# Cross attention with image tokens on one core: the transposes of x placed between the scores and the output projection, and copied out in the same step

## What is computed

```python
q = heads(x @ W_q);  k_t, v_t = heads(text @ W_k), heads(text @ W_v)
probs_t = softmax(q @ k_t.T * scale)                    # 73 text tokens
text_out = probs_t @ v_t
k_ip, v_ip = heads(ip @ W_k_ip), heads(ip @ W_v_ip)     # 4 image tokens
sem = l2norm(probs_t @ text) @ l2norm(ip).T
probs_ip = softmax(q @ k_ip.T * scale + 0.5 * sem) * spatial_mask
out = (text_out + probs_ip @ v_ip) @ W_out + b_out + x
```

## Time and profile before

| | |
|---|---|
| median of 3 runs | 1068.55 us (1067.39 to 1069.84) |
| the profiled execution, its own time | 1065.76 us |
| its span in the profile | 1063.6 us |
| mean granted clock of TensorE | 0.984 of full speed |
| busy: PE, DVE, ACT, POOL | 93%, 77%, 64%, 56% |

### The profile page before, as it was taken

The page is one execution under the profiler, slowest core; times in us unless marked ns, Lnnn a source line. Parts: engine busy times, 40 slices in busy tenths (PEclk is TensorE's granted clock), DMA queues, the critical chain, the costliest instruction groups (busy, mean ns, idle before and its releaser), DMA issues.

```text
span 1063.6 us, 23677 instructions
## 1 busy us (share of the span) xinstructions
PE 988.4 (93%) x7637; PEld 800.9 (75%) x7637; DVE 816.2 (77%) x2397; ACT 677.0 (64%) x1995; POOL 590.6 (56%) x1570
## 2 busy tenths in 40 slices
PE   5996587899998999999998999999999999999967
PEld 4872466688887888888877888888877888888745
DVE  3246378988888888888887888888888888888762
ACT  1124368776776776767766676777766777776630
POOL 0000347766666666756665666666655666666650
PEclk9899799999999999999999999999999999999999
DMA  9598558988889888879798988878898988787852
GB/s 281 167 184 207 124 119 172 156 173 174 168 177 183 172 189 170 184 156 189 156 174 170 185 182 172 174 169 168 167 189 174 188 171 184 142 162 142 156 127 93
DMA packets 484393, 180.56 MB, mean 170 GB/s; under 512 B 451228, under 2 KB 462334, under 8 KB 484271
## 3 DMA queue, kind: packets, MB, share of 16 engines
q1 hardware_dynamic: 484271, 179.07, 81.9%
HBM read 42.74 MB, written 27.22 MB: 66 GB/s over the span
## 4 chain that ended last, share of the span: by engine, by line
PE 73%; DMA 7%; DVE 3%; issue 2%; POOL 2%; ACT 2%; SPq 1%; POOLq 0%; DVEq 0%; ACTq 0%
PE ps_Q L1095 24%; PE ps_O L1061 24%; PE ps_S L1034 11%; PE ps_U L1081 11%; DMA pts<-ph 6%; PE ps_M L1109 3%; ACT pr L818 1%; POOL ph L902 1%; SPq L706 1%; DVE bias L939 1%; ACT ph L830 0%; DMA x_in<-in_x_dram 0%; DMA ipT<-ip 0%; DVE smax L932 0%; DVE pr L972 0%
## 5 line engine op out<-in xcount | busy, mean ns | idle before, releaser
L818 ACT ACTIVATE pr<-ps_S,bias 128x73 f32<-128x73 f32 x1280 | 288.7, 337 | 141.2 <-DVE bias L939 141.2
L902 POOL TENSOR_TENSOR ph<-pr,ph 128x440 f16<-128x440 f32 x320 | 227.8, 733 | 209.2 <-ACT ph L830 209.0
L1061 PE MATMUL ps_O<-wo_hi,aT 128*128 128x320 f16 x1280 | 293.2, 300 | 6.1 <-DVE x_in L924 4.1
L1095 PE MATMUL ps_Q<-xT,wq_hi 128*128 128x512 f32 x800 | 279.8, 415 | 7.0 <-DVE qT L909 6.1
L830 ACT ACTIVATE ph<-pr 128x584 f16<-128x584 f32 x320 | 204.2, 688 | 5.6 <-DMA pts<-ph 0.6
L1061 PE MATMUL ps_O<-wo_lo,aT 128*128 128x320 f16 x640 | 191.3, 299 | 0.0
L1081 PE MATMUL ps_U<-xm,pts 128*128 128x110 f16 (+1 forms) x2560 | 156.6, 213 | 26.4 <-DMA pts<-ph 24.8
L1081 PEld LDWEIGHTS ps_U<-xm,pts 128*128 128x128 f16 (+1 forms) x2560 | 143.4, 98 | 44.4 <-DMA pts<-ph 25.2
L1034 PE MATMUL ps_S<-kbd,qT 128*128 128x308 f32 x960 | 169.7, 312 | 2.8 <-ACT pr L818 2.7
L1095 PEld LDWEIGHTS ps_Q<-xT,wq_hi 128*128 128x128 f32 x800 | 146.0, 190 | 34.9 <-DVE qT L909 7.9
L1061 PEld LDWEIGHTS ps_O<-wo_hi,aT 128*128 128x128 f16 x1280 | 124.8, 98 | 62.9 <-DVE x_in L924 4.8
(11 more groups left out here) (175 smaller groups left out, 1307.0 us busy)
## 6 DMA issues: line engine op xcount, KB each, us to landing
out_dram<-x_in SPq DMA_DIRECT2D x64, 320.0 KB, 3.1
x_in<-in_x_dram SPq DMA_DIRECT2D x60, 320.0 KB, 3.5
w_k<-in_L_xattn_W_k_dram SPq DMA_DIRECT2D x5, 512.0 KB, 9.4
w_ip<-in_L_xattn_W_k_ip_dram SPq DMA_DIRECT2D x1, 2560.0 KB, 12.0
w_v<-in_L_xattn_W_v_dram SPq DMA_DIRECT2D x1, 2560.0 KB, 20.2
w_ip<-in_L_xattn_W_v_ip_dram SPq DMA_DIRECT2D x1, 2560.0 KB, 10.6
pts<-ph SPq DMA_TRANSPOSE x160, 4.4
xm<-x_d SPq DMA_DIRECT2D x20, 110.0 KB
```

What stands on the lines that cost most here:

```text
L818: last = nc.scalar.activation(pr[p % P_RING][:, j, h, :], sc[:, j, h, 0:T], ACT.Exp, bias=bias[p % 2][:, j, h:h + 1], scale=SCALE)
L902: nc.gpsimd.tensor_tensor(lo, full[:, :, t0:t1], one[:, :, 0, t0:t1], ALU.subtract).then_inc(pl_ready, 1)
L1061: last = nc.tensor.matmul(o_bank[half % 2][:, 0:HALF], stationary, moving, start=(k, a, b_) == O_MMS[0], stop=(k, a, b_) == O_MMS[-1])
L1095: last = nc.tensor.matmul(ps_Q[:], wq[a][:, c, k * P:(k + 1) * P], xT[(CC * i + c) % XT_RING][b_][:], start=(c, a, b_) == Q_MMS[0], stop=( ...
```

## The change

On PE the transposes of x are placed behind the scores and ahead of the output projection. ACT and DVE copy them out in the same step, at the same place in their order. The last two chunks of a tile are transposed one step later (places 7 and 8 instead of 6 and 7), so they are copied out in the same steps as before. The first three are transposed in the same steps as before and copied out one step earlier.

```diff
-    XT_AT = {-10: 0, -9: 1, -8: 2, -4: 3, -3: 4}
+    XT_AT = {-10: 0, -9: 1, -8: 2, -3: 3, -2: 4}
...
@@ scalar @@
-                for j, c in x_at(p - 1):
+                for j, c in x_at(p):
                     act.wait_ge(xT_ready, CC * j + c + 1)
...
@@ tensor, behind the scores of the step @@
                     last.then_inc(s_ready, 1)
+
+                for j, c in x_at(p):
+
+                    if c == 0:
+                        pe.wait_ge(x_loaded[j % X_RING], 16 * (SUB * (j // X_RING + 1) if j % X_RING else SUB * (j // X_RING) + 1))
+                    if j:
+                        if m_free is not None:
+                            pe.wait_ge(*m_free)
+                        m_free = xT_lo, CC * j + c + 1
+                    for q in range(SUB):
+                        last = nc.tensor.transpose(x_bank(j, c)[:, q * P:(q + 1) * P],
+                                                   x_in[j % X_RING][:, q, c * P:(c + 1) * P], ident[:])
+                    last.then_inc(xT_ready, 1)
...
@@ tensor, at the end of the step: the same lines, taken out @@
-                for j, c in x_at(p):
...
```

## The result

The changed kernel is slower: 1073.22 us median of 20 runs, against 1069.93 us median of 20 runs before. The ratio is 1.0036, with a 95% interval of 1.0021 to 1.0050, so 3.9 us (2.2 to 5.4); the medians lie 3.3 us apart, the means 3.6. That is beyond the 0.2% that can be told from no change, and inside the range of the forecast (1064.5 to 1074.5). The single figure forecast, 1070.0, a loss of 1.3 us, stood for "no change", and that did not come true.

The account below looks back on a forecast made before the run. PE, with 73% of the last-ending chain, was taken to bound the kernel by its instructions and idle time. Terms 1.2 + 0.5 + 0.9 - 1.3 = 1.3 us lost against 1068.55 gave 1069.9, rounded to 1070.0; range 1064.5 to 1074.5.

Parts of the forecast that it names:

- PE's own time: All 75 moved sets: 0.43 us each ahead of the output projection, net 0; bounds 6 us gained or lost.
- Place 6: Tile's step 6, transposes taken away: next scores wait for exponentials, 0.11 us in 11 steps, 1.2 us lost.
- Places 7 and 8: Set moved within step 7; step 8 grows 0.43 us, place 6's time put elsewhere: 0 in sum.
- Place 2: Transposes ahead of `ps_U` make it 0.35 us later: 0.05 us lost in 11 steps, 0.5 us in all.
- The start: Second tile, step 0: work queued behind the wait for x; step 1's scores 3.5 us late, 0.9 us finally lost.
- The clock: Rival: transposes don't count as busy, so step 1's queries run slowly, 1.4 us more; 1071.4 us, chance 0.07.
- Changes of batch: Steps 42, 82 and 122, place 2: sets fill the last waits for `pts`, 0.43 us each, 1.3 us gained.
- The signs named: Step 1's scores near 132.7, step 16's about 1 us late; a steady step otherwise changed by over 0.1 us means wrong.
- The sum: Whole kernel: 1.2 + 0.5 + 0.9 - 1.3 = 1.3 us lost; no-change outcome given chance 0.45.
- two other slow cases: Start delay never made good, 1072.5 us, chance 0.15; scores waiting for exponentials, 1074.3 us, chance 0.13.
- the one by the exponentials: Rival: scores at places 3 and 7 wait by upper bounds, 2.9 + 3.1 us; 1074.3 us, chance 0.13.

Follow-up runs that it names:

- the turned order at place 7: Changed kernel with DVE's addition L988 ahead of the sum L984 in steps at place 7 alone: 1072.78 us, ratio 1.0032.
- the run with the old start: Changed kernel with the first three sets of the second tile transposed and copied out as before: 1071.70 us, ratio 1.0026.
- a run of its own: Changed kernel with the second tile's first set back behind step 0's queries on PE alone, ACT and DVE copies unchanged: 1077.11 us, ratio 1.0080.
- the third profile of before: Kernel before, unaltered, run again for a third profile of the changes of batch: 1069.21 us, ratio 0.9996.
- An order turned to free one place of the pipeline: Changed kernel with DVE's addition L988 ahead of the sum L984 in all steps: 1082.02 us, ratio 1.0124.

## Why the prediction was right or wrong, point by point

- **PE's own time.** Right. In the changed kernel a set ahead of the output projection takes 0.436 us from its first matmul to the next group's, and scores in front of it 0.85, all as forecast (0.43). Neither bound of 6 us was touched.
- **Place 6.** Right in mechanism and size. Forecast: 0.11 us in each such step. Places 6 and 7 together became 0.23 us shorter, where the 0.35 us taken from place 6 would have made them 0.35 shorter: 0.12 lost. In the changed kernel's step 66 the exponentials end at 498.67 and the next scores start at 498.82.
- **Places 7 and 8: "Place 8 is alike, but its step grows by 0.43, which covers it."** This is the step that failed. DVE's chain at place 7 was taken as a rigid thing that comes 0.35 us later. It is not rigid: 0.35 us later, its addition L988 falls into POOL's work on `ph` and takes 0.87 instead of 0.23 us, `bias` comes 0.7 us later in all (0.33 of it by the collision), and the 0.43 us of cover are used up. Places 8 and 9 grew by 0.57 us where the moved set explains 0.35: 0.22 us lost per tile, 2.0 us over 9.2 tiles, forecast as 0. The kernel before with that one addition made late shows such a loss without any set moved (places 8 and 9 longer by 0.4 to 0.5 us), and the turned order at place 7 takes it away in these two places.
- **Place 2.** Forecast 0.05 us per tile, measured 0.07 to 0.09 (place 0 grew by that much, and place 3 kept its length, where scores without a set in front of them should have saved 0.08). The size was off, and the rows show the same exchange there: L988 takes 0.70 us there (0.21 before), while L1004, which was held up before (0.64), is free (0.23).
- **The start.** Forecast 3.5 us late at step 1, measured 3.7 (step 0: 11.1 and 11.3 against a mean of 7.5). Forecast 0.9 us at step 16. Measured 0.7 in the means against the kernel before, 0.2 to 0.8 against the run with the old start, and 1.1 over all profiles without a further fall of the clock. That exponentials behind the waiting copy hold step 1 up was shown by a run of its own; for the queries behind the waiting transposes there is only the order of the rows. The clock came back after 6.8 us instead of 10.2, as forecast.
- **The clock.** The rule of the Trainium skill's page TensorE: Matmul & The Clock Gate, that transposes do not count as busy time, was weighed and not followed. The changed kernel gives no reason to: there the clock came back earlier, in step 1. But queries and scores ran beside the transposes, so only the 20 transposes of the first tile speak against the rule: at 107.4 us, and more plainly in the third profile of before, where the clock rose while the last of them were still to run (421 ns each, then 272).
- **Changes of batch.** Forecast 1.3 us gained, measured 0.7 (246.7 against 247.4), less than what two profiles of one kernel differ by: not shown. Named nowhere in the forecast: at steps 40 and 120 the set now waits for its load of x, ahead of the output projection. PE's waits for the load of x are 8.1 us in 3 times, 5.7 of them at step 0.
- **The signs named.** Step 1's scores came 11.1 us behind step 0's, so near the 132.7 named (133.1 on that clock). Place 6 became 0.31 us shorter (named: 0.24) and place 8 0.54 longer (named: 0.43), a little over the 0.1 that was to mean "wrong". The short waits of the scores for the exponentials came, at places 3, 7 and 9, though not as a line of their own. The waits for `pts` fell by more than the 2 to 4 us named, but they differ by 6.8 us between profiles of the kernel before. The third change of batch took 81.3 and 80.7 us, against 81.0 to 82.9 before, which shows nothing.
- **The sum.** Forecast 1.2 + 0.5 in the plain steps; measured 3.8 to 4.0 there. The other terms were within 0.6 us. The steps at places 7 and 8, put at 0, make 2.0 of the 2.6 us that were missing. So the forecast was 1.3 us lost, "no change" at 0.45, and the kernel lost 3.9. That the measured time still lies in the range owes something to luck: its upper end was set by two other slow cases, and neither held the mechanism at work. Of the 3.2 us between 1070.0 and 1073.22, 1.4 are the base, since the forecast stood on a median of 3 runs of the kernel before (1068.55) and 20 runs gave 1069.93. Of the rivals, the one by the exponentials was closest: scores do wait for exponentials more often, at places 3, 7 and 9. Its price stood on the upper bounds at 3 and 7 and left 9 out, and what made the exponentials late was not in it.

## What to carry to other kernels

When an instruction is moved, its neighbours on other engines shift against each other, and a shift of a third of a microsecond is not passed on as it is. Look for pairs of engines that hold each other up (here DVE instructions with two inputs from SBUF and POOL), and ask whether the shift moves one of them into the other's time. And where a change puts a wait on a load ahead of other work, ask what is queued behind it on every engine, once for the steady state and once for the first time through.

## What the runs showed that I had not expected

- L988 takes 0.22 us alone and 0.87 to 0.99 us when it starts behind POOL's 1 us subtraction on `ph`. The first of POOL's two instructions takes 1.00 us there, and in each of the three rows shown (504.52, 495.70 and 500.36) L988 ends 0.07 to 0.09 us behind that: with POOL's start at 504.31, for one, at 505.39 against 505.31. The Trainium skill (SBUF — State Buffer, SBUF: two separate sides) has the rule: a DVE instruction with two SBUF inputs and a GpSimd instruction that reads SBUF take an exclusive lock, and the later one waits for the whole of the other. The rows here agree, also in that the sum of L984, with one input from SBUF, keeps its 0.76 us when the turned order at place 7 puts it beside the same work of POOL.
- An order turned to free one place of the pipeline cost 9 us, with the loss in two others.
- PE's short waits are nearly invisible in the list of waits: 5 times for exponentials, 3.8 us, none of them in the plain stretches. The idle time of the weight loads of the scores (12.2 to 28.6 us, most of it "issue") showed them.
- Between executions of one kernel, the prologue varies from 121.3 to 123.6 us, the three changes of batch by 2.7 us in sum, and the stretch behind step 159 from 49.2 to 54.1 us. Two profiles are not enough for an effect of 1 to 3 us in such a stretch.
